# Four score banks, 512-column up products, and the key stack's reads on GpSimd's queue

## The chip, the cores and the metric

The kernel runs on one core of a Trainium2 chip. The metric is the device time of one execution in microseconds (us), the median of several runs. The core's engines each work through their own instructions in order: TensorE (PE, matrix products into eight banks of PSUM), VectorE (DVE), ScalarE (ACT), GpSimd (POOL) and SyncE (SP, which here only issues transfers). They wait for each other by semaphores.

## The reference

Sixteen sequences of 256 tokens, 256 wide, pass through four layers, each conditioned on a vector of 64 per sequence:

```python
h = gamma * rmsnorm(x) + beta                       # layer 0, attention, 16 heads of width 16
o = softmax(scale * q @ k.T) @ v
x = x + alpha * (o @ W_o.T)
x = x + f_alpha * (silu(h2 @ gate.T) * (h2 @ hidden.T) @ out_w.T + out_b)
u = (x * (scale * rsqrt(ms + eps))) @ up_w.T        # layer 1, up product 256 -> 2048
val, gate = split(u)
x = quantised(val * gelu(gate)) @ ternary(down_w).T + x
x = x + relu(x @ Wd_b + bd) @ Wu_b + bu             # layer 2, adapter with per-sequence weights
x = layernorm(x) * w + b, with tanh(cond @ lin_w) added   # layer 3
```

## The kernel before

Each sequence is one batch of the program, and three batches are in flight: `run(a, f, g, nxt)` does the attention of batch a, the feed-forward part and the up product of batch f = a - 1, and the down product, adapter and layer norm of batch g = a - 2; it also prepares q, k and v of batch nxt = a + 1. Every engine has its own `run` with the same four arguments. The order of work on each engine is written out by hand, and `whole` calls `run` for batches 0, 1 and 2, then in a loop for 3 to 14, then for 15, and then `drain`. I call one `run` a pass.

On TensorE a pass is: eight gate products (L650, 12 matmuls each), with the max products (L593), the output products (L664) and the transposes of the quantised rows (L706) between them; then the score stage: down products (L713), 16 heads of scores (L609, two matmuls of 256 columns a head), norm_g (L674) and four attends (L619, 16 small matmuls for four heads), with the pieces of batch g (L720, L727, L733) and `project_v` of nxt (L576) between; then q and k of nxt (L567), mean (L553), output projection (L627), means (L553, L636), `project_v` (L576) again; then eight groups of the up product (L695, 12 matmuls of 256 columns each: two halves, three products, two chunks).

A head's scores go to one of three banks (`SCORE_BANKS`, chosen by h % 3), and ScalarE turns them into probabilities (`exps`, L1005) in one of seven slots. So head h waits for the exponential of head h - 3, attend t for the exponentials of heads 4t to 4t + 3, and the exponential of a head from 7 on for an attend that gives its slot free:

```python
if h >= 3:
    pe.wait_ge(s_exp.sem, s_exp.at(b, h - 2))
...
if h >= SLOTS:
    act.wait_ge(pv_mm.sem, pv_mm.at(b, (h - SLOTS) // 4 + 1))
```

VectorE normalises the attended values in two halves (`normalise`, L1323 to L1331, and `normalised`, L1337 to L1341): half 0 after attends 0 and 1, half 1 after attends 2 and 3. `relu` (L1474) of batch g stands ahead of half 0. In the up product, group n waits for VectorE's `gated_u` (L1411) of group n - 2, since two banks take turns.

q and k are split into a high and a low part and go through memory: SyncE's `stack_qk` writes `q_dram` and `k_dram` (L332), waits until both are there, and reads them back in another layout, six transfers for `q_stack` (L345) and six for `k_stack` (L353), of 128 rows of 1 KB each. Behind them on SyncE stand the output of batch g (L410), which waits for GpSimd's `layer_out` (L472 to L477), and the loads of the next pass (x_in at L317 and others). GpSimd's pass is: eight differences `act_lo` (L495), the adapter's weights (L511), `layer_out`.

Of the kernel before, what the change touches and what calls it, by code (L numbers as in the profile page):

```python
# [22 lines left out]
P = 128  # L23
# [12 lines left out]
SCORE_BANKS = (0, 1, 5)  # L36
# [42 lines left out]
def build(nc, xT, condT, w_cond, w_qkvT, w_oT, w_ghT, w_outT, out_b, w_upT, w_downT,  # L79
          w_hyper, head_rows, adapt_w, adapt_b, bd, bu, ln_w, ln_b, lin_b, ident_in, out):  # L80
    with ExitStack() as ctx:
# [149 lines left out]
        qk_dram_w, stack_dma = sem("qk_dram_w", 32), sem("stack_dma", 16 * 14)  # L231
# [78 lines left out]
        with nc.Block() as block:  # L310

            @block.sync
            def _(sp):
# [7 lines left out]
                def stack_qk(b):  # L321

                    for x, dram in enumerate((q_dram, k_dram)):
# [3 lines left out]
                        if b.follows():  # L327
                            left_value = known(sp, stack_dma.at(b, back=1))
                            sp.wait_ge(stack_dma.sem, left_value)
# [16 lines left out]
                    for a in range(2):  # L346
                        even = slice(64 * a, 64 * a + 32, 2)
                        odd = slice(64 * a + 1, 64 * a + 32, 2)
                        third = slice(64 * a + 32, 64 * a + 64, 2)
                        for rows_at, part in ((even, 0), (odd, 0), (third, 1)):  # L350
                            src = k_dram[:, part].rearrange("(m a r) n -> a r m n", a=2, r=DH)[a]
                            to = k_stack[rows_at].rearrange("r (m a) n -> r a m n", a=2)[:, a]
                            sp.dma_start(to.bitcast(F32), src).then_inc(stack_dma.sem, 16)  # L353
# [113 lines left out]
            def _(pool):  # L467
# [11 lines left out]

                def low_part(n):  # L480
# [7 lines left out]
                def run(a, f, g, nxt):  # L488
# [16 lines left out]
                    if g:  # L505
# [5 lines left out]
                        pool.tensor_tensor(adapt[:], adapt[:], adapt_base[:], ALU.add).then_inc(adapt_w_ready.sem, 1)  # L511
                        layer_out(g)
# [30 lines left out]
                pool.wait_ge(stack_dma.sem, stack_dma.at(Batch(0)))  # L543
                for n in range(2, 10):
                    hyper_load(n)
# [4 lines left out]
            def _(pe):  # L550
# [29 lines left out]
                def max_scores(b, n):  # L580
                    pair, qt = n // 2, n % 2
                    if n == 0:
                        pe.wait_ge(stack_dma.sem, stack_dma.at(b))

# [17 lines left out]
                def scores(b, h):  # L602
# [3 lines left out]
                    if h >= 3:  # L606
                        pe.wait_ge(s_exp.sem, s_exp.at(b, h - 2))
                    for k in range(TT):
                        mm = pe.matmul(halves(SCORE_BANKS[h % 3])[:, k, :], k_stack[:, h, k * P:(k + 1) * P], q_stack[:, h // 2, :],  # L609
                                       start=True, stop=True)  # L610
# [67 lines left out]
                def up(b, n):  # L678
# [11 lines left out]
                    at = halves(7 - n % 2)  # L690
                    for x in range(2):
                        i = 0
                        for w, h in ((up_hi, h3_hi), (up_lo, h3_hi), (up_hi, h3_lo)):
                            for d in range(DC):
                                mm = pe.matmul(at[:, x, :], h[:, d, t * P:(t + 1) * P],  # L695
                                               w[:, d, x * F + c * UW:x * F + (c + 1) * UW], start=(i == 0), stop=(i == 5))
                                i += 1
# [63 lines left out]
                def run(a, f, g, nxt):  # L761
# [46 lines left out]
                    for t in range(4):  # L808
                        if a:
                            if t == 2 and f:  # L810
                                pe.wait_ge(n3_dve.sem, n3_dve.at(f))
                            if t < 3:
                                scores(a, 4 * t + 5)
                                scores(a, 4 * t + 6)
                            elif nxt:
                                project_v(nxt, 0)
# [7 lines left out]
                        if a:  # L824
                            for h in range(4 * t + 7, min(4 * t + 9, H)):
                                scores(a, h)
# [129 lines left out]
            def _(act):  # L956
# [42 lines left out]
                def exps(b, h):  # L999
# [5 lines left out]
                    act.activation(probs[:, h % SLOTS], halves(SCORE_BANKS[h % 3]), ACT.Exp, scale=float(H / D) ** 0.5).then_inc(s_exp.sem, 1)  # L1005
# [116 lines left out]
                def run(a, f, g, nxt):  # L1122
                    if starts(a):
                        act.wait_ge(stack_dma.sem, stack_dma.at(a))
# [655 lines left out]
```

## Time and profile before

| | |
|---|---|
| time, median of 3 runs | 1068.99 us (1067.8 to 1069.29) |
| the profiled execution | 1068.02 us, of which the span of the trace is 1066.2 us |
| TensorE busy | 993.7 us, 93% of the span, 7442 matmuls |
| TensorE weight loads | 848.0 us, 80% |
| VectorE, ScalarE, GpSimd busy | 750.6 us (70%), 553.9 us (52%), 192.7 us (18%) |
| mean granted clock of TensorE | 0.96 of full speed; full in the loop |
| the chain that ended last, by engine | PE 74%, issue 9%, DVE 6%, ACT 4%, DMA 3% |

A row of a timeline has its start in us from the span's start, its length in us, the engine, the line of the kernel, the operation, what it writes and reads (program names), how many instructions it merges (x), and in brackets the idle time before it with what ended it. Matmuls are pipelined, and their ends are modelled: a row's length is longer than what it costs the next one, so the distance from one start to the next is the thing to read. "PE" rows are matmuls; "SPq" rows are transfers as SyncE issues them.

### The profile page before, as it was taken

How to read it: one execution, taken by the hardware profiler on the slowest of the kernel's cores; microseconds unless marked ns; L12 is line 12 of the kernel's file. 1: busy time of each engine (PE TensorE's matmuls, PEld its weight loads, DVE VectorE, ACT ScalarE, POOL GpSimd, SP SyncE). 2: the span in 40 equal slices, each digit the busy share in tenths (PEclk: the TensorE clock that was granted, in tenths of full speed). 3: DMA queues.
4: the chain of work that ended last, by engine and by line, in shares of the span. 5: the costliest groups of instructions: out<-in, count | busy, mean ns of one | idle time of the engine just before them, and what ended most of it. 6: DMA issues, size and time to landing. Idle time of an engine off the chain costs nothing.

```text
span 1066.2 us, 22449 instructions
## 1 busy us (share of the span) xinstructions
PE 993.7 (93%) x7442; PEld 848.0 (80%) x7442; DVE 750.6 (70%) x1720; ACT 553.9 (52%) x1166; POOL 192.7 (18%) x246
## 2 busy tenths in 40 slices
PE   5586989999999999999999999999999999998995
PEld 4244759798898979798988979797988979796984
DVE  3725468676777778686777878686767778785645
ACT  3163364655555464656555463646555564645532
POOL 1411421112020201111120201021120202021220
PEclk9576989999999999999999999999999999999997
DMA  8994543040402113040403112030404022130000
GB/s 287 287 343 129 208 149 91 2 140 2 132 8 90 49 45 94 1 139 1 139 1 110 29 62 77 23 116 1 139 1 129 11 80 60 40 90 2 21 21 10
DMA packets 78321, 89.45 MB, mean 84 GB/s; under 512 B 18688, under 2 KB 64912, under 8 KB 75664
## 3 DMA queue, kind: packets, MB, share of 16 engines
q1 hardware_dynamic: 72640, 63.86, 20.1%
q0 software_dynamic: 2304, 16.78, 4.3%
q10 hardware_dynamic: 3344, 8.39, 2.2%
q8 instruction: 19, 0.31, 0.1%
q14 instruction: 14, 0.11, 0.0%
HBM read 63.14 MB, written 25.31 MB: 83 GB/s over the span
## 4 chain that ended last, share of the span: by engine, by line
PE 74%; issue 9%; DVE 6%; ACT 4%; DMA 3%; POOL 1%; SPq 1%; ACTq 0%; DVEq 0%; POOLq 0%
PE bank L695 15%; PE bank L650 15%; PE bank L664 7%; PE bank L619 6%; PE bank L609 5%; PE bank L593 5%; PE bank L567 4%; PE bank L553 3%; PE bank L713 2%; PE bank L576 2%; ACT probs L1005 2%; PE bank L756 2%; PE bank L636 1%; PE bank L727 1%; PE bank L674 1%
## 5 line engine op out<-in xcount | busy, mean ns | idle before, releaser
L1005 ACT ACTIVATE probs<-bank 128x512 f32<-128x512 f32 x256 | 139.6, 598 | 54.9 <-PE bank L609 54.1
L1306 DVE TENSOR_REDUCE neg_max<-bank 128x2 f32<-128x512 f32 x256 | 161.8, 680 | 0.5 <-PE bank L593 0.5
L495 POOL TENSOR_TENSOR act_lo<-act_f,act_hi 128x256 fp32r<-128x256 f32 x120 | 89.7, 753 | 393.4 <-ACT act_hi L1048 393.4
L1042 ACT ACTIVATE silu_g<-bank 128x256 f32<-128x256 f32 x128 | 49.2, 385 | 192.6 <-PE bank L650 192.4
L1084 ACT ACTIVATE gelu_g<-bank,r 128x256 f32<-128x256 f32 x128 | 60.8, 475 | 95.6 <-PE bank L695 94.8
L609 PE MATMUL bank<-q_stack,k_stack 128*128 128x256 f32 x512 | 99.0, 317 | 11.9 <-ACT probs L1005 11.0
L695 PE MATMUL bank<-up_hi,h_hi 128*128 128x256 f32 x512 | 108.7, 294 | 0.9 <-DVE y L1279 0.3
L650 PE MATMUL bank<-h_hi,gh_hi 128*128 128x256 f32 x512 | 103.7, 284 | 4.6 <-DVE h_lo L1367 4.6
L650 PE MATMUL bank<-h_lo,gh_hi 128*128 128x256 f32 x512 | 103.3, 283 | 0.0
L695 PE MATMUL bank<-up_lo,h_hi 128*128 128x256 f32 x512 | 103.1, 283 | 0.0
L650 PE MATMUL bank<-h_hi,gh_lo 128*128 128x256 f32 x512 | 102.9, 283 | 0.0
L695 PE MATMUL bank<-up_hi,h_lo 128*128 128x256 f32 x512 | 100.7, 278 | 0.0
L1373 DVE TENSOR_TENSOR act_f<-bank,silu_g 128x256 f32<-128x256 f32 x128 | 53.5, 418 | 62.9 <-ACT silu_g L1042 62.9
L609 PEld LDWEIGHTS bank<-q_stack,k_stack 128*128 128x128 f32 x512 | 73.8, 196 | 29.1 <-ACT probs L1005 21.7
L593 PE MATMUL bank<-k_stack,q_stack 128*128 128x512 f32 x256 | 87.6, 429 | 8.9 <-DMA k_stack<-k_dram 6.8
L650 PEld LDWEIGHTS bank<-h_hi,gh_hi 128*128 128x128 f32 x512 | 82.0, 190 | 11.7 <-issue 8.3
L1411 DVE TENSOR_TENSOR act_u<-bank,gelu_g 128x256 f32<-128x256 f32 x128 | 54.1, 422 | 48.1 <-ACT gelu_g L1084 46.1
L472 POOL TENSOR_TENSOR xc<-xc,y 128x512 f32<-128x512 f32 x15 | 19.4, 1295 | 362.2 <-DVE y L1279 362.2
L695 PEld LDWEIGHTS bank<-up_hi,h_hi 128*128 128x128 f32 x512 | 79.3, 189 | 5.3 <-DVE act_u L1411 3.5
L695 PEld LDWEIGHTS bank<-up_lo,h_hi 128*128 128x128 f32 x512 | 79.8, 192 | 0.0
L695 PEld LDWEIGHTS bank<-up_hi,h_lo 128*128 128x128 f32 x512 | 79.2, 190 | 0.0
L650 PEld LDWEIGHTS bank<-h_hi,gh_lo 128*128 128x128 f32 x512 | 79.1, 190 | 0.0
(190 smaller groups left out, 2138.6 us busy)
## 6 DMA issues: line engine op xcount, KB each, us to landing
hyper<-w_hyper POOLq DMA_DIRECT2D x16, 1024.0 KB, 6.5
q_stack<-q_dram SPq DMA_DIRECT2D x96, 128.0 KB
k_stack<-k_dram SPq DMA_DIRECT2D x96, 128.0 KB
q_dram<-probs SPq DMA_DIRECT2D x16, 512.0 KB, 2.8
k_dram<-probs SPq DMA_DIRECT2D x16, 512.0 KB, 3.6
x_res<-xT SPq DMA_DIRECT2D x16, 256.0 KB, 2.8
x_in<-xT SPq DMA_DIRECT2D x15, 256.0 KB, 2.7
out<-xc SPq DMA_DIRECT2D x15, 256.0 KB, 2.5
```

The costliest lines, as they stand in the source:

```text
L495: pool.tensor_tensor(act_lo[:, c % 3, :], act_f[:, c % 2, :], act_hi[:, c % 3, :].bitcast(F32), ALU.subtract).then_inc(g_lo.sem, 1)
L593: pe.matmul(bank[n % 3][:], q_stack[:, pair, qt * P:(qt + 1) * P], k_stack[:, 2 * pair:2 * pair + 2, :], start=True, stop=True).then_inc(m ...
L609: mm = pe.matmul(halves(SCORE_BANKS[h % 3])[:, k, :], k_stack[:, h, k * P:(k + 1) * P], q_stack[:, h // 2, :], start=True, stop=True)
L619: mm = pe.matmul(at[32 * j:32 * j + 32, t % 2, :], v_aug[:, k, 4 * t + j, :], probs[:, (4 * t + j) % SLOTS, k, :], start=(k == 0), stop=(k ...
L650: mm = pe.matmul(at[:, x, :], w[:, d, x * F + c * P:x * F + (c + 1) * P], h[:, d, :], start=(n == 0), stop=(n == 5))
L664: mm = pe.matmul(halves(3)[:, m, :], w[:, c, m * P:(m + 1) * P], h[:, c % 3, :], start=(c == 0 and m == 0 and n == 0), stop=(c == FC - 1 a ...
L695: mm = pe.matmul(at[:, x, :], h[:, d, t * P:(t + 1) * P], w[:, d, x * F + c * UW:x * F + (c + 1) * UW], start=(i == 0), stop=(i == 5))
L1005: act.activation(probs[:, h % SLOTS], halves(SCORE_BANKS[h % 3]), ACT.Exp, scale=float(H / D) ** 0.5).then_inc(s_exp.sem, 1)
L1084: act.activation(gelu_g[:, n % 2, :], halves(7 - n % 2)[:, 1, :], ACT.Gelu, scale=r3[:, t:t + 1])\
L1306: dve.tensor_reduce(neg_max[:, qt, :, pair:pair + 1].rearrange("p a o -> p (a o)"), halves(n % 3), AX_X, ALU.max, negate=True).then_inc(ma ...
L1373: dve.tensor_tensor(act_f[:, c % 2, :], halves(4 + c % 2)[:, 1, :], silu_g[:, c % 2, :], ALU.mult)\
L1411: dve.tensor_tensor(act_u[:, t, c * UW:(c + 1) * UW], halves(7 - n % 2)[:, 0, :], gelu_g[:, n % 2, :], ALU.mult).then_inc(u_dve.sem, 1)
```

## The change

Five edits go together.

1. The up product's two halves (values and gates) become one matmul of 512 columns, whose moving operand is two runs of 256 columns. A group has 6 matmuls and not 12.
2. Scores use four banks: a table gives each head its bank (0, 1, 5 for the first six heads, then 4 as well). From head 7 on a head waits for the exponential of head h - 4 (before: h - 3); head 6 waits until VectorE has read bank 4 in the norm of batch nxt. Heads 5 to 7 go ahead of attend 0, 8 to 11 ahead of attend 1, 12 to 15 ahead of attend 2.
3. From batch 1 on the six reads of `k_stack` are issued by GpSimd (`read_k`), behind the adapter's weights and ahead of `layer_out`, after a small operation and waits for the last scores of batch a and for both writes to memory. Batch 0's stay with SyncE, with a semaphore of their own.
4. SyncE's writes of q_dram and k_dram wait for the last max product of the batch before instead of for the stack's reads.
5. VectorE's `relu` stands inside `normalise(a, 0)`, behind the shuffle.

```diff
-SCORE_BANKS = (0, 1, 5)
+SCORE_BANKS = (0, 1, 5, 0, 1, 5, 4, 0, 1, 5, 4, 0, 1, 5, 4, 0)
...
+            def stack_k(eng, count):
+                for a in range(2):
+                    even = slice(64 * a, 64 * a + 32, 2)
+                    odd = slice(64 * a + 1, 64 * a + 32, 2)
+                    third = slice(64 * a + 32, 64 * a + 64, 2)
+                    for rows_at, part in ((even, 0), (odd, 0), (third, 1)):
+                        src = k_dram[:, part].rearrange("(m a r) n -> a r m n", a=2, r=DH)[a]
+                        to = k_stack[rows_at].rearrange("r (m a) n -> r a m n", a=2)[:, a]
+                        eng.dma_start(to.bitcast(F32), src).then_inc(count.sem, 16)
...
-                            left_value = known(sp, stack_dma.at(b, back=1))
-                            sp.wait_ge(stack_dma.sem, left_value)
+                            left_value = known(sp, max_mm.at(b, back=1))
+                            sp.wait_ge(max_mm.sem, left_value)
...
+                    if not b.follows():
+                        stack_k(sp, first_k_dma)
...
+                def read_k(b):
+                    pool.wait_ge(s_mm.sem, s_mm.at(b, back=1))
+                    pool.wait_ge(qk_dram_w.sem, qk_dram_w.at(b))
+                    pool.tensor_tensor(pool_idle, pool_idle, pool_idle, ALU.mult)
+                    stack_k(pool, k_stack_dma)
...
+                    if nxt:
+                        read_k(nxt)
+                    if g:
                         layer_out(g)
...
+                        if b.follows():
+                            pe.wait_ge(k_stack_dma.sem, k_stack_dma.at(b, back=1))
...
-                    if h >= 3:
-                        pe.wait_ge(s_exp.sem, s_exp.at(b, h - 2))
+                    if h >= 3 and h != 6:
+                        pe.wait_ge(s_exp.sem, s_exp.at(b, h - (2 if h < 6 else 3)))
+                    if h == 6 and nxt:
+                        pe.wait_ge(n1_dve.sem, n1_dve.at(nxt, 4))
                     for k in range(TT):
-                        mm = pe.matmul(halves(SCORE_BANKS[h % 3])[:, k, :], k_stack[:, h, k * P:(k + 1) * P], q_stack[:, h // 2, :],
+                        mm = pe.matmul(halves(SCORE_BANKS[h])[:, k, :], k_stack[:, h, k * P:(k + 1) * P], q_stack[:, h // 2, :],
...
-                    at = halves(7 - n % 2)
-                    for x in range(2):
-                        i = 0
-                        for w, h in ((up_hi, h3_hi), (up_lo, h3_hi), (up_hi, h3_lo)):
-                            for d in range(DC):
-                                mm = pe.matmul(at[:, x, :], h[:, d, t * P:(t + 1) * P],
-                                               w[:, d, x * F + c * UW:x * F + (c + 1) * UW], start=(i == 0), stop=(i == 5))
-                                i += 1
+                    i = 0
+                    for w, h in ((up_hi, h3_hi), (up_lo, h3_hi), (up_hi, h3_lo)):
+                        for d in range(DC):
+                            both = w[:, d, :].rearrange("p (x f) -> p x f", x=2)[:, :, c * UW:(c + 1) * UW]
+                            mm = pe.matmul(halves(7 - n % 2), h[:, d, t * P:(t + 1) * P], both, start=(i == 0), stop=(i == 5))
+                            i += 1
...
-                            if t < 3:
-                                scores(a, 4 * t + 5)
-                                scores(a, 4 * t + 6)
-                            elif nxt:
+                            if t == 0:
+                                for h in range(5, 8):
+                                    scores(a, h, nxt)
+                            elif t == 3 and nxt:
                                 project_v(nxt, 0)
                             attend(a, t)
...
-                        if a:
-                            for h in range(4 * t + 7, min(4 * t + 9, H)):
+                        if a and t < 2:
+                            for h in range(4 * t + 8, 4 * t + 12):
                                 scores(a, h)
...
+                    if between:
+                        relu(between)
```

How the edits move instructions is shown at two places. The first is TensorE in the loop's score stage, from the stage's norm to attend 2. Before (L609 scores, L619 attend, L720, L727, L733 pieces of batch g; a head of scores is two matmuls; products in full precision, the attend's among them, are listed here with half the number that the trace has, 8 for 16):

```order
L609 MATMUL bank<-q_stack,k_stack 128x256 x4
L619 MATMUL bank<-probs,v_aug 32x256 x8
L720 MATMUL bank<-ident,mlp_y 128x128 x4
L609 MATMUL bank<-q_stack,k_stack 128x256 x8
L619 MATMUL bank<-probs,v_aug 32x256 x8
L724 REGISTER_ALU
L727 MATMUL bank<-x,adapt 128x256 x2
L609 MATMUL bank<-q_stack,k_stack 128x256 x4
L811 REGISTER_ALU
L609 MATMUL bank<-q_stack,k_stack 128x256 x4
L619 MATMUL bank<-probs,v_aug 32x256 x8
L733 MATMUL bank<-adapt_h,adapt 128x256 x2
```

After (L630 scores, L640 attend, L739, L746, L752 the same pieces):

```order
L630 MATMUL bank<-q_stack,k_stack 128x256 x2
L628 ISA
L630 MATMUL bank<-q_stack,k_stack 128x256 x4
L640 MATMUL bank<-probs,v_aug 32x256 x8
L739 MATMUL bank<-ident,mlp_y 128x128 x4
L630 MATMUL bank<-q_stack,k_stack 128x256 x8
L640 MATMUL bank<-probs,v_aug 32x256 x8
L743 REGISTER_ALU
L746 MATMUL bank<-x,adapt 128x256 x2
L630 MATMUL bank<-q_stack,k_stack 128x256 x8
L830 REGISTER_ALU
L640 MATMUL bank<-probs,v_aug 32x256 x8
```

One head more stands ahead of attend 0, and the last head, which stood behind L733, now stands ahead of attend 2; the other heads are the same four between two attends.

The second place is GpSimd at the end of its pass in the loop. Before (L511 adapter's weights, L472 to L477 `layer_out`):

```order
L495 TENSOR_TENSOR act_lo<-act_f,act_hi 128x256 x2
L510 ISA
L511 TENSOR_TENSOR adapt<-adapt,adapt_base 128x512
L471 ISA
L472 TENSOR_TENSOR xc<-xc,y 128x512
L474 ISA
L475 TENSOR_TENSOR columns<-columns 128x1
L477 TENSOR_SCALAR xc<-xc,neg_w,par_g 128x256 x2
```

After (L522 adapter's weights, L321 the reads of k, L477 to L482 `layer_out`):

```order
L506 TENSOR_TENSOR act_lo<-act_f,act_hi 128x256 x2
L521 ISA
L522 TENSOR_TENSOR adapt<-adapt,adapt_base 128x512
L486 ISA
L487 ISA
L488 TENSOR_TENSOR columns<-columns 128x1
L321 DMA k_stack<-k_dram 16x8x256 x6
L476 ISA
L477 TENSOR_TENSOR xc<-xc,y 128x512
L479 ISA
L480 TENSOR_TENSOR columns<-columns 128x1
L482 TENSOR_SCALAR xc<-xc,neg_w,par_g 128x256 x2
```

Two waits, a small operation and six transfers stand between the adapter's weights and `layer_out`. SyncE has lost the same six.

## Rows read from the trace of the kernel before

**Rows 1.** TensorE's timeline: the first max products of two neighbouring passes.

```profile
528.64 0.86 PE L593 MATMUL bank<-k_stack,q_stack 128*128 128x512 f32 x3
...
588.02 0.85 PE L593 MATMUL bank<-k_stack,q_stack 128*128 128x512 f32 x3
```

**Rows 2.** TensorE's timeline in the score stage of the same pass.

```profile
554.11 0.72 PE L609 MATMUL bank<-q_stack,k_stack 128*128 128x256 f32 x4
554.76 1.07 PE L619 MATMUL bank<-probs,v_aug 128*32 128x256 f32 x16
...
556.17 0.96 PE L609 MATMUL bank<-q_stack,k_stack 128*128 128x256 f32 x6
557.42 0.50 PE L609 MATMUL bank<-q_stack,k_stack 128*128 128x256 f32 x2 [0.29 <-ACT probs L1005]
557.85 1.07 PE L619 MATMUL bank<-probs,v_aug 128*32 128x256 f32 x16
558.85 1.13 PE L727 MATMUL bank<-x,adapt 128*128 128x256 f32 x4
559.63 1.05 PE L609 MATMUL bank<-q_stack,k_stack 128*128 128x256 f32 x6
560.98 0.50 PE L609 MATMUL bank<-q_stack,k_stack 128*128 128x256 f32 x2 [0.30 <-ACT probs L1005]
561.42 1.07 PE L619 MATMUL bank<-probs,v_aug 128*32 128x256 f32 x16
...
564.58 1.07 PE L619 MATMUL bank<-probs,v_aug 128*32 128x256 f32 x16
565.58 3.72 PE L567 MATMUL bank<-h,w_qkv 128*128 128x256 f32 x16
```

**Rows 3.** ScalarE's timeline in the same stage.

```profile
560.33 0.60 ACT L1005 ACTIVATE probs<-bank 128x512 f32<-128x512 f32 x1 [1.11 <-PE bank L609]
...
561.23 1.56 ACT L1005 ACTIVATE probs<-bank 128x512 f32<-128x512 f32 x3
562.66 0.43 ACT L1009 ACTIVATE den_y<-den 128x256 f32<-128x256 f32 x1
```

**Rows 4.** VectorE's timeline in the same pass.

```profile
552.66 0.69 DVE L1288 TENSOR_TENSOR h<-x_in,bank 128x512 f32<-128x512 f32 x1
...
560.42 0.48 DVE L1323 TENSOR_SCALAR den_raw<-bank,rows_of 128x256 f32<-128x256 f32 x1
...
565.72 0.48 DVE L1323 TENSOR_SCALAR den_raw<-bank,rows_of 128x256 f32<-128x256 f32 x1
...
578.95 0.42 DVE L1411 TENSOR_TENSOR act_u<-bank,gelu_g 128x256 f32<-128x256 f32 x1
...
580.46 0.70 DVE L1367 TENSOR_TENSOR h_lo<-h,h_hi 128x512 fp32r<-128x512 f32 x1
```

**Rows 5.** The chain that ended last: start, length, matmuls of 256 and of 512 columns.

```profile
527.38 1.43 PE bank L650 x12
528.81 0.70 PE bank L593 x3
```

**Rows 6.** SyncE's queue, as it issues the reads of q and the next x_in.

```profile
575.93 3.88 SPq L345 DMA_DIRECT2D q_stack<-q_dram  x6
...
584.92 0.40 SPq L317 DMA_DIRECT2D x_in<-xT  x1
```

**Rows 7.** GpSimd's timeline: four issues at the start, and the output stage of the pass.

```profile
39.60 2.15 POOL L532 DMA_DIRECT2D hyper<-w_hyper  x4 [1.78 <-DMA k_stack<-k_dram]
...
575.75 1.29 POOL L472 TENSOR_TENSOR xc<-xc,y 128x512 f32<-128x512 f32 x1 [25.29 <-DVE y L1279]
```

**Rows 8.** VectorE's timeline at the start, while GpSimd works too.

```profile
39.57 0.48 DVE L1722 TENSOR_SCALAR adapt_bias<-w_early,w_stats 128x512 f32<-128x512 f32 x1
...
80.45 1.37 DVE L1339 SCALAR_TENSOR_TENSOR den_x<-den_x,den_y 128x256 f32<-128x256 f32 x1
```

**Rows 9.** ScalarE's timeline: the first use of x_in in the next pass.

```profile
590.68 0.62 ACT L958 ACTIVATE h<-x_in 128x512 f32<-128x512 f32 x1
```

**Rows 10.** The page's list of transfers: issues, KB each, us to landing.

```profile
x_in<-xT SPq DMA_DIRECT2D x15, 256.0 KB, 2.7
```

More of the change, by code:

```diff
@@ L230, in build @@
         x_in_dma, x_res_dma = sem("x_in_dma", 32), sem("x_res_dma", 32)
-        qk_dram_w, stack_dma = sem("qk_dram_w", 32), sem("stack_dma", 16 * 14)
+        qk_dram_w, stack_dma = sem("qk_dram_w", 32), sem("stack_dma", 16 * 8)
+        first_k_dma, k_stack_dma = sem("first_k_dma"), sem("k_stack_dma", 16 * 6)
         max_dma = sem("max_dma", 32)
@@ L345, in stack_qk @@
                             sp.dma_start(q_stack[rows_at].bitcast(F32), src).then_inc(stack_dma.sem, 16)
[L346 to L353, printed above, removed]
+                    if not b.follows():
+                        stack_k(sp, first_k_dma)
                 def load_res(b):
@@ L543, in _ @@
                 pool.wait_ge(stack_dma.sem, stack_dma.at(Batch(0)))
+                pool.wait_ge(first_k_dma.sem, 16 * 6)
                 for n in range(2, 10):
@@ L583, in max_scores @@
                         pe.wait_ge(stack_dma.sem, stack_dma.at(b))
+                        if b.follows():
+                            pe.wait_ge(k_stack_dma.sem, k_stack_dma.at(b, back=1))
+                        else:
+                            pe.wait_ge(first_k_dma.sem, 16 * 6)
                     if n == 0:
@@ L600, in max_turn, with scores @@
                     mm.then_inc(max_t.sem, 1)
-                def scores(b, h):
+                def scores(b, h, nxt=None):
                     if h == 0:
@@ L1004, in exps @@
                         act.wait_ge(pv_mm.sem, pv_mm.at(b, (h - SLOTS) // 4 + 1))
-                    act.activation(probs[:, h % SLOTS], halves(SCORE_BANKS[h % 3]), ACT.Exp, scale=float(H / D) ** 0.5).then_inc(s_exp.sem, 1)
+                    act.activation(probs[:, h % SLOTS], halves(SCORE_BANKS[h]), ACT.Exp, scale=float(H / D) ** 0.5).then_inc(s_exp.sem, 1)
                 def den_guess(b, u):
@@ L1124, in run @@
                         act.wait_ge(stack_dma.sem, stack_dma.at(a))
+                        act.wait_ge(first_k_dma.sem, 16 * 6)
                         raw_load(2)
@@ L1307, in row_max, with normalise @@
                                       negate=True).then_inc(max_red.sem, 1)
-                def normalise(b, u):
+                def normalise(b, u, between=None):
                     k = 8 * u
@@ L1525, in run @@
                         norm_g(f)
-                    if g:
+                    if g and not a:
                         relu(g)
@@ L1531, in run @@
                     if a:
-                        normalise(a, 0)
+                        normalise(a, 0, g)
                     if starts(a):
```

## Prediction

> **What bounds the kernel now.** I read the page first (TensorE is the full engine), then TensorE's timeline through one pass of the loop, then ScalarE's, VectorE's and the queues' at the same place. The passes in the middle look alike, so one stands for all: the first wide max product of two neighbouring passes starts at 528.64 and 588.02, a period of 59.4 us [rows 1]. TensorE is the bound, but it isn't always working. From the first attend (554.76) to the projection L567 (565.58) it spends 10.82 us [rows 2]. The reader is to see two holes there, at 557.42 and 560.98, each ended by ScalarE's exponential. The brackets give 0.29 and 0.30 us, but the ends of matmuls are modelled; by starts, the three heads from 556.17 (six matmuls of 0.12) were through by 556.9 and the next one began at 557.42. ScalarE itself waits at the same places, because head 7 is issued only behind attend 0 and the transpose L720 (and head 11 behind attend 1 and L727): each engine idles in turn for the other. With three banks TensorE can't run far enough ahead to fill this.
>
> **The score order.** Distances between starts give block lengths [rows 2]: attend 1.00 (557.85 to 558.85), L727 0.78, L720 0.41 (from 554.76 to 556.17 less an attend), two heads of scores with their start-up 0.65, each further head 0.24, so four heads some 1.1. From attend 2 to attend 3 it is 3.16: an attend, head 15 (0.41), and 1.75 for L733 and L576. I lay the new order on the clock of this pass:
> - heads 5, 6, 7 from 554.11 take 0.89: attend 0 at 555.00 (0.24 later than before), L720 at 556.00;
> - heads 8 to 11 from 556.41: attend 1 at 557.50 (before 557.85), L727 at 558.50;
> - heads 12 to 15 from 559.28: attend 2 at 560.4 (before 561.42);
> - L733 and L576, then attend 3 at 563.15 (before 564.58), L567 at 564.15 (before 565.58).
> That is 1.4 to 1.5, and I take 1.5, since blocks that now adjoin lose some of the start-up that I counted twice.
>
> Is ScalarE there in time? Exponentials in a row come every 0.48 (three in 1.56) and L1075 between adds 0.4 (560.33 to 561.23) [rows 3]. Head 11's needs attend 1 to be over, 558.6. Then L1075 and, once head 12 is there (about 559.8), three exponentials until 561.3, the pair L1009/L1011 (two of 0.43) until 562.2, and the last until 562.8. Attend 3 at 563.15 finds it done, with 0.3 spare. VectorE: the first normalisation starts when attend 1 is over, 558.6 instead of 560.42, 1.8 earlier; the relu that now stands inside it adds 0.4 to 0.5, as L1323's 0.48. So the second (5.30 after the first [rows 4]) starts 1.3 to 1.4 earlier, about when attend 3 is over. What is late next is therefore VectorE's chain, by 0.1 or 0.2; TensorE has L567 and L553 to do before it needs the result, so I let the 1.5 pass. The new wait of head 6 on bank 4 is for L1288, the last reader of that bank, which ends at 553.35 [rows 4], before 554.11: nothing.
>
> **The up products.** 96 matmuls of 256 columns become 48 of 512 per batch. Twelve of 256 take 1.43, 0.119 each; three of 512 with new weights each take 0.70, 0.233 each [rows 5]. A pair of 0.238 becomes 0.233: 48 x 0.005, or 0.24 to 0.3 per batch. The fourth group of products waits for VectorE's L1411, which ends at 579.37 [rows 4] at the end of VectorE's own chain of norms. So what the first three of eight groups save is given back there: 0.2 per pass are left. The Trainium skill (TensorE: Matmul & The Clock Gate, Back-to-back issue gap) gives a gap of N/2.4 + 2.5 ns, by which a pair saves only 2.5 ns. By it this term would be 0.1 in place of 0.2, and the whole some 1 us slower; the rows show 0.119 and 0.233, both above its 0.109 and 0.216, so I stay with the rows.
>
> **The key reads.** SyncE now issues 6 reads of q (3.88 us from 575.93) and not 12; six of k go to GpSimd, with a small operation ahead, and the output stage L472 and its followers stand behind them there. Nothing waits for the stack in the loop: the twelfth read was out by 583.7, and the first product that needs them starts at 588.02 with no idle before it [rows 1]. So taking them away from SyncE brings nothing by itself; the question is whether GpSimd's issues hurt. The trace has no k read from GpSimd. Nearest row: four of the 1 MB hyper loads in 2.15, 0.54 each [rows 7]. The bound from above: SyncE takes 0.65 for a q read and 0.40 for x_in [rows 6], so the finer pattern may cost 1.6 times as much, 0.9. I take 0.54 to 0.9, near the first because both are 128 rows. From 574.6 (575.93 less 1.5, plus the small operation) six end at 577.8 to 580.0. Behind them wait L472 (at 575.75 before), L475 and L477, 2.6 in all (L472 1.29 of it [rows 7]), so xc is ready at 580.5 to 582.6, not 578.4. Who waits for that is SyncE, with the output and behind it x_in, which was issued at 584.92. SyncE itself has 3.8 us of reads fewer ahead of it, so x_in goes out at 582 to 584, not later than now in the pass. ScalarE wants it at 590.68 [rows 9]. Cost: nothing. If GpSimd takes 1.35 per issue, that cover is gone: 574.6 + 8.1 + 2.6 + 1.0 for output and x_in, and 2.7 to land [rows 10] is 589.0, its new due time (590.68 less 1.7).
>
> **Sum.** 13 passes with all three batches in flight, 1.7 each: 22.1. The passes of batches 0, 1 and 15 have the same four attends, but hyper products, table loads or VectorE's chain between: 1.5 each, 4.5; their up products and those of the drain, 0.3 each, 0.9. Batch 1's k reads in the start land earlier by some 3 us, but gate products stand ahead of their use: 0. Together 27.5 from 1068.0 of the profiled execution (1.0 under the median of the runs): 1040.5, and 1041 for the median.
>
> **Rivals.**
> - Collision on VectorE's and GpSimd's port, chance 0.13. At 80.45 a VectorE operation with two inputs from the tile memory took 1.37 for 256 elements (L1323 takes 0.48), about as long as GpSimd's own operations, one of which was in flight [rows 8]. L1367 (580.46 [rows 4], so 579.0 in the new pass) is of that kind. If the issues cost 0.65 to 0.85, L472 starts just ahead of it, its 1.29 hold it up, and the product of up group 3 behind it comes 0.65 late, so TensorE stops: 13 x 0.65 = 8.5, 1049. Outside this span of costs L472 falls before or after it.
> - The stall only moves, chance 0.12: ScalarE or VectorE, with 0.3 and nothing spare, end the stage later than laid out, and 0.9 of the 1.5 is left. 16 x 0.9 + 3.5 = 18, 1050.
> - GpSimd's issues are slow: slower than before, chance 0.06. From 1.35 each on, every 0.1 costs 0.6 per pass; at 1.65 the 1.7 is used up and it decides. At 2.0 it is 2.1 x 13 = 27 over, 1095. Against it stands the 0.54 row, and that VectorE kept to 0.48 for L1722 right then (39.57) [rows 8]. The Trainium skill (SBUF — State Buffer, the "DVE blocks DMA" trap) says that VectorE's fast modes keep GpSimd from writing descriptors; if that rule bites it is this case, and in the rows of 39.57 and 39.60 it doesn't.
> - The change doesn't do what it says, chance 0.03: what ends the stage is the chain of norms and the reorder is absorbed, 1067 to 1069.
> - Better than laid out, chance 0.06: the start-ups of the score blocks go too, 2.0 per pass, and up keeps all of its 0.3: 13 x 2.3 + 6 = 36, 1032.
>
> **How the numbers follow.** The likeliest case, chance 0.60, gives 1041, by itself 1036 to 1046. The range for 8 in 10 takes in the two rivals of 1049 and 1050 and not the far ones: 1034 to 1052. Faster by over 0.2% (about 2 us, what a measurement of this kernel can tell from none) is all but the slow issues, part of which is still a gain, and the fourth case: 0.90. Same 0.04, slower 0.06.
>
> **What would show it.** Right: passes of 57.7; L609 with no idle before it by ScalarE; four attends closer, L567 some 9.2 after attend 0; the up matmuls of 512 every 0.23; GpSimd's six issues within 3.2 to 5.4 us. Wrong: an idle of TensorE ahead of L553 or the up products that VectorE ends (rivals 1 and 2); ScalarE waiting for x_in, or the first max product for k_stack (rival 3). My forecast fails most easily in the cost of GpSimd's issues and in ScalarE's 0.3 us of slack.

## The result, and the profile after

The changed kernel took **1052.14 us** (median of 4 runs, 1048.5 to 1052.55) and the kernel before 1068.65 beside it: ratio 0.9832, 95% interval 0.9811 to 0.9852. That is 16.5 us faster. The profiled execution took 1052.55, with a span of 1051.0. I had forecast 27.5 us of gain, so the direction is right and the size is not: 11 us are missing. The time lies at the slow end of my range (1034 to 1052).

The page of the changed kernel, busy time of each engine and the lines on scores, products and transfers:

```profile
PE 983.8 (94%) x6674; PEld 803.0 (76%) x6674; DVE 753.2 (72%) x1720; ACT 554.0 (53%) x1166; POOL 247.3 (24%) x351
...
L630 PE MATMUL bank<-q_stack,k_stack 128*128 128x256 f32 x512 | 84.8, 304 | 3.5 <-ACT probs L1024 3.5
...
k_stack<-k_dram POOLq DMA_DIRECT2D x90, 128.0 KB, 4.9
...
x_in<-xT SPq DMA_DIRECT2D x15, 256.0 KB, 3.7
out<-xc SPq DMA_DIRECT2D x15, 256.0 KB, 4.1
```

Scores now wait 3.5 us for exponentials in the whole run; 11.0 of the 11.9 us of idle that L609 had before were ended so. The lines have new numbers: L609 is L630, attend L619 is L640, L567 is L582, L576 is L591, L727 and L733 are L746 and L752, the up products L695 are L715, the exponentials L1005 are L1024, the output stage L472 is L477.

TensorE's timeline: the first max products of two neighbouring passes, and the first gate products of batch 1 and of batch 14, between which lie all 13 passes with three batches in flight:

```profile
172.69 0.40 PE L671 MATMUL bank<-h_hi,gh_hi 128*128 128x256 f32 x2
...
522.99 0.87 PE L612 MATMUL bank<-k_stack,q_stack 128*128 128x512 f32 x3
...
581.15 0.87 PE L612 MATMUL bank<-k_stack,q_stack 128*128 128x512 f32 x3
...
928.96 0.40 PE L671 MATMUL bank<-h_hi,gh_hi 128*128 128x256 f32 x2
```

The period is 58.16 here, where it was 59.38 [rows 1]. The 13 passes take 756.27, or 58.17 each. The same two products stand in the trace of before at:

```profile
171.28 0.40 PE L650 MATMUL bank<-h_hi,gh_hi 128*128 128x256 f32 x2
...
943.00 0.40 PE L650 MATMUL bank<-h_hi,gh_hi 128*128 128x256 f32 x2
```

That is 771.72, or 59.36 each. So a pass is 1.19 shorter and 13 of them 15.4, where I had 22.1. All but about 1 us of the measured gain is there.

TensorE's timeline of the changed kernel in the score stage (it answers to [rows 2]):

```profile
548.45 0.96 PE L630 MATMUL bank<-q_stack,k_stack 128*128 128x256 f32 x6
549.34 1.07 PE L640 MATMUL bank<-probs,v_aug 128*32 128x256 f32 x16
550.34 0.66 PE L739 MATMUL bank<-ident,mlp_y 128*128 128x128 f32 x4
550.75 1.19 PE L630 MATMUL bank<-q_stack,k_stack 128*128 128x256 f32 x8
551.88 1.07 PE L640 MATMUL bank<-probs,v_aug 128*32 128x256 f32 x16
552.88 1.13 PE L746 MATMUL bank<-x,adapt 128*128 128x256 f32 x4
553.66 1.30 PE L630 MATMUL bank<-q_stack,k_stack 128*128 128x256 f32 x8
554.88 1.07 PE L640 MATMUL bank<-probs,v_aug 128*32 128x256 f32 x16
555.88 1.13 PE L752 MATMUL bank<-adapt_h,adapt 128*128 128x256 f32 x4
556.85 1.03 PE L591 MATMUL bank<-w_qkv,h 128*128 128x256 f32 x4
557.81 1.07 PE L640 MATMUL bank<-probs,v_aug 128*32 128x256 f32 x16
558.81 3.72 PE L582 MATMUL bank<-h,w_qkv 128*128 128x256 f32 x16
```

The reader is to see the four attends 2.54, 3.00 and 2.93 apart and no bracket anywhere: the trace shows no wait of TensorE here. Yet the stage, from attend 0 to L582, is 9.47 and not the 9.2 that I named.

ScalarE's timeline at its end:

```profile
554.28 1.58 ACT L1024 ACTIVATE probs<-bank 128x512 f32<-128x512 f32 x3 [0.27 <-PE bank L630]
...
556.51 0.58 ACT L1024 ACTIVATE probs<-bank 128x512 f32<-128x512 f32 x1
```

The last exponential is through at 557.09, 0.7 ahead of attend 3. ScalarE is not what made the stage longer than I laid it out.

GpSimd's timeline, from the key reads to the output stage, and SyncE's queue at the same time:

```profile
569.20 0.19 POOL L488 TENSOR_TENSOR columns<-columns 128x1 f32<-128x1 f32 x1 [24.41 <-DMA k_dram<-probs]
569.33 3.24 POOL L321 DMA_DIRECT2D k_stack<-k_dram  x6
572.58 1.31 POOL L477 TENSOR_TENSOR xc<-xc,y 128x512 f32<-128x512 f32 x1
573.96 0.53 POOL L480 TENSOR_TENSOR columns<-columns 128x1 f32<-128x1 f32 x1
```

```profile
569.15 3.88 SPq L356 DMA_DIRECT2D q_stack<-q_dram  x6
575.76 0.40 SPq L415 DMA_DIRECT2D out<-xc  x1
576.72 0.40 SPq L328 DMA_DIRECT2D x_in<-xT  x1
```

Six issues in 3.24, 0.54 each, and x_in goes out at 576.72 where it is first wanted at 583.83 (a row of ScalarE's timeline, below).

```profile
583.83 0.62 ACT L977 ACTIVATE h<-x_in 128x512 f32<-128x512 f32 x1
```

### The profile page after: what moved, and what is told of

Same layout as the page of the kernel before. It is cut to its first block, busy times and chain, and to the rows that moved or that the text cites. A ratio compares the mean times of both kernels' runs of the same rounds, so it can differ in the third digit from the quotient of the medians.

```text
span 1051.0 us, 20966 instructions
## 1 busy us (share of the span) xinstructions
PE 983.8 (94%) x6674; PEld 803.0 (76%) x6674; DVE 753.2 (72%) x1720; ACT 554.0 (53%) x1166; POOL 247.3 (24%) x351
## 4 chain that ended last, share of the span: by engine, by line
PE 75%; DVE 8%; issue 7%; DMA 5%; ACT 2%; POOL 1%; SPq 1%; ACTq 0%; DVEq 0%; POOLq 0%
PE bank L671 16%; PE bank L715 13%; PE bank L685 8%; PE bank L630 6%; PE bank L640 6%; PE bank L612 5%; PE bank L582 5%; PE bank L568 3%; PE bank L732 3%; PE bank L591 2%; PE bank L695 1%; PE bank L746 1%; PE bank L752 1%; PE bank L775 1%; DMA par_a<-cond_dram 1%
## 5 line engine op out<-in xcount | busy, mean ns | idle before, releaser
L1024 ACT ACTIVATE probs<-bank 128x512 f32<-128x512 f32 x256 | 139.7, 598 | 28.3 <-PE bank L630 22.5
L630 PE MATMUL bank<-q_stack,k_stack 128*128 128x256 f32 x512 | 84.8, 304 | 3.5 <-ACT probs L1024 3.5
L715 PE MATMUL bank<-up_hi,h_hi 128*128 128x512 f32 x256 | 87.1, 422 | 1.1 <-DVE act_u L1433 0.2
L488 POOL TENSOR_TENSOR columns<-columns 128x1 f32<-128x1 f32 x15 | 2.9, 193 | 346.5 <-DMA k_dram<-probs 346.5
L715 PE MATMUL bank<-up_lo,h_hi 128*128 128x512 f32 x256 | 80.3, 395 | 0.0
L715 PE MATMUL bank<-up_hi,h_lo 128*128 128x512 f32 x256 | 80.3, 395 | 0.0
L671 PEld LDWEIGHTS bank<-h_lo,gh_hi 128*128 128x128 f32 x512 | 79.1, 189 | 0.0
L630 PEld LDWEIGHTS bank<-q_stack,k_stack 128*128 128x128 f32 x512 | 69.2, 195 | 12.2 <-ACT probs L1024 7.1
L685 PE MATMUL bank<-act_hi,fo_hi 128*128 128x256 f32 x256 | 75.5, 295 | 0.9 <-POOL act_lo L506 0.7
L685 PE MATMUL bank<-act_hi,fo_lo 128*128 128x256 f32 x256 | 71.4, 279 | 0.0
```

What stands on the lines that cost most here:

```text
L630: mm = pe.matmul(halves(SCORE_BANKS[h])[:, k, :], k_stack[:, h, k * P:(k + 1) * P], q_stack[:, h // 2, :], start=True, stop=True)
L671: mm = pe.matmul(at[:, x, :], w[:, d, x * F + c * P:x * F + (c + 1) * P], h[:, d, :], start=(n == 0), stop=(n == 5))
L685: mm = pe.matmul(halves(3)[:, m, :], w[:, c, m * P:(m + 1) * P], h[:, c % 3, :], start=(c == 0 and m == 0 and n == 0), stop=(c == FC - 1 a ...
L715: mm = pe.matmul(halves(7 - n % 2), h[:, d, t * P:(t + 1) * P], both, start=(i == 0), stop=(i == 5))
L1024: act.activation(probs[:, h % SLOTS], halves(SCORE_BANKS[h]), ACT.Exp, scale=float(H / D) ** 0.5).then_inc(s_exp.sem, 1)
```

## The experiments

Single executions of one kernel lie up to 8.5 us apart, so each kernel is read in two ways: its ratio to the kernel before on the same chip, and the 13 passes in its trace (first gate product of batch 1 to that of batch 14). The second is far sharper: three traces of the changed kernel give 756.27, 756.31 and 756.48, so a difference of 0.02 us in a pass can't be told from none. In the table, "A" is the time up to that first product (it holds the attends of batches 0 and 1) and "C" what follows the last (it holds those of batch 15).

| kernel | ratio (95% interval) | A | 13 passes | one pass | C |
|---|---|---|---|---|---|
| before | 1 | 171.3 | 771.7 | 59.36 | 123.2 |
| e1, up products alone | 0.9993 (0.9981 to 1.0006) | 171.6 | 770.6 | 59.27 | 124.5 |
| e2, score part alone | 0.9850 (0.9825 to 0.9876) | 170.7 | 757.5 | 58.27 | 121.5 |
| e3, key reads alone | 0.9993 (0.9981 to 1.0006) | 171.8 | 772.0 | 59.38 | 122.9 |
| e4, up and scores | 0.9826 (0.9805 to 0.9847) | 171.0 | 756.1 | 58.16 | 121.1 |
| e11, e4 again | 0.9836 (0.9809 to 0.9862) | 173.0 | 756.0 | 58.15 | 123.5 |
| after | 0.9832 (0.9811 to 0.9852) | 172.7 | 756.3 | 58.17 | 122.0 |
| e5, after again | 0.9844 (0.9820 to 0.9868) | 172.7 | 756.3 | 58.18 | 122.0 |
| e12, after again | 0.9830 (0.9801 to 0.9860) | 172.0 | 756.5 | 58.19 | 123.7 |
| e10, first keys on SyncE | 0.9815 (0.9790 to 0.9841) | 170.5 | 756.5 | 58.19 | 122.7 |
| e7, e4 with three banks | 1.0002 (0.9984 to 1.0019) | 172.1 | 771.1 | 59.32 | 122.6 |
| e8, e4 in the old order | 0.9866 (0.9843 to 0.9888) | 171.7 | 759.6 | 58.43 | 122.6 |
| e9, e4 with relu ahead | 0.9876 (0.9851 to 0.9900) | 171.7 | 759.4 | 58.42 | 122.7 |
| e6, e4 with the modulations split off | 0.9790 (0.9762 to 0.9818) | 172.0 | 752.4 | 57.88 | 123.1 |

**e1: the up products alone.** The kernel before with only this hunk:

```
-                    for x in range(2):
-                        ...
-                                mm = pe.matmul(at[:, x, :], h[:, d, t * P:(t + 1) * P],
+                            both = w[:, d, :].rearrange("p (x f) -> p x f", x=2)[:, :, c * UW:(c + 1) * UW]
+                            mm = pe.matmul(halves(7 - n % 2), h[:, d, t * P:(t + 1) * P], both, start=(i == 0), stop=(i == 5))
```

> The kernel before with the 512-wide up products alone. My term for this part was 0.3 x 16 = 4.5 at most and 0.2 per pass at the least, so 3 to 4.5 us of gain. The trace of the changed kernel shows only 0.09 us per pass gained between the first up product and the next gate, because more up groups now wait for VectorE's gated product: by that theory (VectorE eats the gain) this kernel is 1 to 2 us faster than before, 1067. Rival, the gain is all there and was given back elsewhere in the changed kernel: 4 us, 1064.5.

1068.44 against 1068.83, and 0.09 us per pass. The rival (the whole gain of 4 us) is out: the interval ends at 2 us.

**e2: the score part alone.** The kernel before with the bank list, the waits, the order of heads and attends, and the relu of the diff; nothing else.

```
-SCORE_BANKS = (0, 1, 5)
+SCORE_BANKS = (0, 1, 5, 0, 1, 5, 4, 0, 1, 5, 4, 0, 1, 5, 4, 0)
-                    if g:
+                    if g and not a:
                         relu(g)
```

> The kernel before with four score banks, the new order of scores and attends, and relu moved behind the shuffle; up products stay 256 wide and all stack reads stay on SyncE's queue. Theory: this part alone is what the change gained, 1.1 us in each of 14 to 15 batches (15 to 17 us), so 1052 to 1054, with the period 58.25 to 58.3. Rival, the start of the run lost 1.5 to 3 us to the key reads that ran beside the query reads: then this kernel has what the changed kernel has in its loop and does not pay that, 1050 to 1052.

1052.04, and 1.10 us per pass, as expected. This part is the gain.

**e3: the key reads alone.** From batch 1 on they are issued by GpSimd, and SyncE's writes have the new wait (edit 4); scores, banks, relu and up products as before.

```
+                    if nxt:
+                        read_k(nxt)
+                    if g:
                         layer_out(g)
```

> The kernel before with the key reads from batch 1 on issued from GpSimd's queue, nothing else. Theory from the prediction: nothing, 1068 to 1069. Rival: batch 1's query stack lands 7.1 us after its issue (so in the changed kernel's trace) because the key reads run beside it, and the maxima of batch 1 start some 2 us later: 1070 to 1071, with the loop's period unchanged at 59.4.

1068.61 against 1068.83, and 0.02 us per pass more, about as much as traces of one kernel differ. The interval of this run, start and end of the run included, leaves the key reads a cost of at most 0.6 us beside the old scores; the rival (1.2 to 2.2 us) is out. The three parts add up: 0.09 + 1.10 - 0.02 = 1.17, and the changed kernel has 1.19.

**e4: up and scores, keys on SyncE.** The changed kernel with this undone:

```
-                    if nxt:
-                        read_k(nxt)
+                    for a in range(2):
+                        ...
+                            sp.dma_start(to.bitcast(F32), src).then_inc(stack_dma.sem, 16)
```

> The changed kernel with its key reads left on SyncE's queue: wide up products and the score part. If the key reads cost nothing it takes what the changed kernel took, 1052 within 0.5. If they cost the start of the run some 2 us, it takes 1050.

1050.09, which looked like 2 us for the key reads. The passes say otherwise (58.16 and 58.17); what differs is A and C. That was put to the test with the next runs.

**e5, e11, e12 and e10: do the key reads cost anything at the ends?** e5 and e12 are the changed kernel, e11 is e4 once more on the chip of e12, and e10 gives back to SyncE only the reads of batch 1:

```
-                    if not b.follows():
+                    if b.early():
                         stack_k(sp, first_k_dma)
...
-                    if nxt:
+                    if nxt and not nxt.early():
                         read_k(nxt)
```

> The changed kernel itself once more, beside the other runs of this group. The kernel with the same wide products and score part but the key reads on SyncE took 1050.1, this one took 1052.1, on different chips. If the key reads cost the start of the run, it stays at 1052, with the second batch's last gate stage (the third in the run) starting 1.5 to 2 us later (172.7 against 171.0). If that was only the run's own variation, 1050 to 1051.

> Wide up products and the score part with the key reads on SyncE, once more, on the same chip as the changed kernel. If the key reads on GpSimd cost something, 1050 again and the changed kernel 2 to 3 us above it; if the difference was between chips, both the same within 0.5.

> The changed kernel beside it: 1052 to 1053.5 if the key reads cost something, else as the one with the keys on SyncE within 0.5.

> The changed kernel with the second batch's key reads issued by SyncE as before; GpSimd reads the keys from the third batch on. The changed kernel took 1052.1 and 1053.5, with the keys on SyncE 1050.1. Theory: the difference is made at the second batch, where the input of the next batch, behind the query reads, landed 7.0 us after its issue and not 3.0: this kernel takes 1050 to 1051. Rival: it is made in the end or is variation, and this kernel takes what the changed kernel takes beside it.

1053.48 for e5, whose first gate product of batch 1 stands at 172.67 as in the first trace of this kernel. That looked like the theory, but e11, with the keys on SyncE, has it at 173.01. On one chip the medians are 1050.63 (e10), 1051.98 (e11) and 1052.82 (e12). The last two differ by 0.8, with intervals of the ratio that overlap almost wholly: no cost of the key reads that these runs can tell from none. e10 is lower than e12 as the first theory had it, by 2.2 us, but e11 has those reads on SyncE as well and is lower by only 0.8; the interval of e10 overlaps both. With the new scores, a cost of a microsecond at batch 1 is neither shown nor excluded.

What is seen to differ with A and C, between traces of one kernel, is the granted clock. Two traces of one and the same kernel, e4 and e11, by windows (stretch, its length and busy TensorE with its instructions, then the granted clock):

```profile
960.00:970.00 10.00, 6.58 (x49) 0.94 0.01 2
970.00:980.00 10.00, 9.59 (x35) 0.89 0.08 27
```

```profile
960.00:970.00 10.00, 6.59 (x61) 0.92 0.01 2
970.00:980.00 10.00, 9.64 (x29) 0.74 0.00 1
```

Both have full clock (2.4 GHz) up to 960 and lose it around the stretch in which TensorE worked 6.6 of 10 us; e11 gets less of the next ten at full clock, and its C is 2.4 us longer. By these two rows 1.5 us of that can be the clock (an estimate: 0.15 of ten us). A goes the same way: from 100 to 110 us the clock is 0.83 in e4 and 0.66 in e11, from 140 to 150 it is 0.87 and 0.71. In e11 the projection of batch 0 stands 0.8 us earlier (89.90 against 90.71), the first scores of batch 1 0.8 later (135.20 against 134.37) and its projection 2.0 later (157.22 against 155.19).

**e7: three banks in the new order.** e4 with

```
-SCORE_BANKS = (0, 1, 5, 0, 1, 5, 4, 0, 1, 5, 4, 0, 1, 5, 4, 0)
+SCORE_BANKS = (0, 1, 5)
-                    if h >= 3 and h != 6:
-                        pe.wait_ge(s_exp.sem, s_exp.at(b, h - (2 if h < 6 else 3)))
+                    if h >= 3:
+                        pe.wait_ge(s_exp.sem, s_exp.at(b, h - 2))
```

> The same but with only three score banks in the new order of heads and attends. Theory: the fourth bank is what makes the new order work. From the exponentials' ends, head 7 would wait 0.1, head 11 0.5 and head 15 0.4 us for the exponential three heads back, 1.0 us per batch: 1064 to 1066, a period of 59.2. Rival, the order alone brings the gain: 1050 to 1052.

1068.13 against 1068.47: nothing is left of the gain, where I had expected 0.16 us of each pass to stay (59.32 and not 59.2). TensorE's timeline shows the holes back, now ahead of heads 11 and 15 (in the kernel before, ahead of 10 and 14):

```profile
557.20 0.96 PE L609 MATMUL bank<-q_stack,k_stack 128*128 128x256 f32 x6
558.46 0.50 PE L609 MATMUL bank<-q_stack,k_stack 128*128 128x256 f32 x2 [0.30 <-ACT probs L1003]
558.90 1.07 PE L619 MATMUL bank<-probs,v_aug 128*32 128x256 f32 x16
...
560.68 1.05 PE L609 MATMUL bank<-q_stack,k_stack 128*128 128x256 f32 x6
561.95 0.50 PE L609 MATMUL bank<-q_stack,k_stack 128*128 128x256 f32 x2 [0.22 <-ACT probs L1003]
```

**e8: four banks in the old order.** e4 with the heads issued in pairs again:

```
-                            if t == 0:
-                                for h in range(5, 8):
-                                    scores(a, h, nxt)
+                            if t < 3:
+                                scores(a, 4 * t + 5, nxt)
+                                scores(a, 4 * t + 6, nxt)
```

> The same with four score banks but the old order of heads and attends. Theory: TensorE's two holes of 0.3 us (ahead of heads 9 and 13) close, since these heads no longer wait for an exponential that has just begun; the time that ScalarE idles for heads 7 and 11 stays: half of the gain, 0.5 to 0.6 us per batch, 1057 to 1059. Rival, the idle of ScalarE decides and the attends stay where they were: 1066.

1055.10 and 58.43 per pass. Less the 0.09 of the up products, 0.84 of the score part's 1.10 is there (with the relu in its new place), more than I expected. The order is worth the other 0.27, and by itself, with three banks (e7), nothing. The holes that close are those ahead of heads 10 and 14, not 9 and 13 as the expectation has it. In this kernel ScalarE's timeline keeps two idles, ahead of the exponentials of heads 7 and 11, that the new order removes:

```profile
551.59 0.60 ACT L1005 ACTIVATE probs<-bank 128x512 f32<-128x512 f32 x1 [0.67 <-PE bank L611]
...
554.72 0.60 ACT L1005 ACTIVATE probs<-bank 128x512 f32<-128x512 f32 x1 [0.68 <-PE bank L611]
```

**e9: relu ahead of the first normalisation.** e4 with

```
-                    if g and not a:
+                    if g:
                         relu(g)
...
-                        normalise(a, 0, g)
+                        normalise(a, 0)
```

> Wide up products, four banks, new order, key reads on SyncE, and VectorE's relu back ahead of the first normalisation. There it waits for the product L727, which ends 1.0 us after attend 1, so the reciprocal's input is ready 1.0 later. ScalarE issues the last exponential behind that reciprocal; it ends at 555.34 where attend 3 begins at 556.06, 0.72 of slack. Theory: attend 3 comes 0.2 to 0.3 later, 3 to 4 us in all, 1053 to 1054, with the period 58.4. Rival: the slack takes it, 1050.

1055.48, 58.42 per pass, 0.26 longer: the size in a pass is as expected, the reason is not. TensorE's and VectorE's timelines:

```profile
556.31 1.13 PE L733 MATMUL bank<-adapt_h,adapt 128*128 128x256 f32 x4
557.46 1.10 PE L576 MATMUL bank<-w_qkv,h 128*128 128x256 f32 x4
558.49 1.07 PE L621 MATMUL bank<-probs,v_aug 128*32 128x256 f32 x16
```

```profile
556.83 0.48 DVE L1333 SCALAR_TENSOR_TENSOR o_norm<-bank,rows_of,o_norm 128x256 f32<-128x256 f32 x1
```

The last exponential still ends (557.80) 0.7 ahead of attend 3. It is L576 that is late. It writes bank 2, which the normalisation reads until L1333 is over (557.31), and L576 starts 1.15 after L733, where it is 0.97 in e4 (554.13 to 555.10). With relu inside (e4), L1333 was over 1.0 us ahead of L576.

**e6: the modulations split off.** e4, with the two modulations behind the normed x1 moved behind VectorE's second gated product:

```
+                def modulated_f(b):
                     dve.wait_ge(n2_dve.sem, n2_dve.at(b, 4))
...
                         if a and n == 0:
                             scaled_f(a)
+                        if a and n == 1:
+                            modulated_f(a)
```

> Wide up products and the score part with the key reads on SyncE, and on VectorE the two modulations behind the normed x1 moved behind the second gated product of the up stage. Theory: the fourth up group is late by 0.27 us and the fifth by 0.1 because the second gated product stands behind all three operations (570.40 where its Gelu ended at 569.88). Freed, each pass is 0.3 shorter: 57.9 instead of 58.2, and 4 to 5 us in all, 1045.5 to 1046.5. Rival: the next product waits for something else in its place (ScalarE's pair of copies, then its rounded copy), 1050.

1048.52, 57.88 per pass: 0.28 shorter, as expected, and the fastest kernel of the study, 2.1% under before. The whole time is 2 us above the 1045.5 to 1046.5 that I expected, since I counted from e4's 1050.09; e11, the same kernel as e4, took 1051.98 on another chip. Below, TensorE's timeline of the changed kernel at the start of its third, fourth and fifth up group, and of e6 at the same three:

```profile
570.96 0.69 PE L715 MATMUL bank<-up_hi,h_hi 128*128 128x512 f32 x2
...
572.63 0.73 PE L715 MATMUL bank<-up_hi,h_hi 128*128 128x512 f32 x2
...
574.13 0.62 PE L715 MATMUL bank<-up_hi,h_hi 128*128 128x512 f32 x2
```

```profile
568.75 0.69 PE L696 MATMUL bank<-up_hi,h_hi 128*128 128x512 f32 x2
...
570.20 0.61 PE L696 MATMUL bank<-up_hi,h_hi 128*128 128x512 f32 x2
...
571.57 0.63 PE L696 MATMUL bank<-up_hi,h_hi 128*128 128x512 f32 x2
```

1.67 and 1.50 apart in the one, 1.45 and 1.37 in the other. What held the fourth group was VectorE's second gated product, which stood behind three operations on h2.

## Why the prediction was right in sign and 11 us off in size

- **What bounds, and that the holes close.** Right. Both holes of 0.3 are gone, two of 0.30 and 0.22 come back when the fourth bank is taken away (e7), and the score part by itself makes the gain (e2).
- **"I take 1.5."** Mis-sized, and the main error: the score stage gives 1.10 per pass (e2), and 0.4 times 13 is 5.2 us. I laid the stage out with block lengths from other neighbourhoods, and the timeline after shows which were short. Heads 12 to 15 took 1.22 (553.66 to 554.88), heads 8 to 11 1.13, where I had "some 1.1". L752 to L591 took 0.97 where I used 0.78, the length of a block like it with scores behind it; with L591 at 0.96 my 2.75 for attend 2 to attend 3 became 2.93. Attend 0 came 0.24 later, as said, so the gain in front of L567 is that from attend 0 on, 1.35, less 0.24: 1.11. My own layout gave 1.43; the rest was my rounding up to 1.5 with a reason (start-up counted twice) that had the wrong sign. Of the blocks that now adjoin, none got shorter here, and two got longer.
- **ScalarE in time with 0.3 to spare.** Right, with 0.7 to spare.
- **VectorE's chain late by 0.1 or 0.2, hidden by L567 and L553.** In a pass of the loop it is 4.42 from L567 to the projection L627 in both traces (565.58 to 570.00 before, 558.81 to 563.23 after): hidden. What I didn't see is what the relu's place is worth. I priced it inside the normalisation as 0.4 to 0.5 on a covered chain; ahead of it, it would have held L591 through bank 2, 0.26 per pass (e9).
- **Up products, "0.24 to 0.3 per batch", 0.2 in a pass.** Mis-sized. In the traces a group of up products that waits for nothing takes 1.41 before (576.38 to 577.79) and 1.39 after (569.57 to 570.96), so eight give 0.16. I had taken 0.119 from the gate products' row; those of the up stage were 0.1175 apart. Of the 0.16, 0.07 is given back, nearly all at the fourth group, whose wait for VectorE grew, as I had said (its predecessor takes 1.67 with that wait, 0.28 over a group without a wait; in the kernel before it took 1.63, 0.22 over). 0.09 is left (e1), 1.4 us less in 13 passes than forecast. The rule of the Trainium skill that the prediction set aside (TensorE: Matmul & The Clock Gate, Back-to-back issue gap) would have given 0.1 and was nearer than my two rows. What it gets right is the difference of a pair; the distances themselves are above it here too (0.1175 and 0.232 for its 0.109 and 0.216).
- **The key reads cost nothing.** Right in the loop (e3: 0.02 per pass; e4 and e11 within 0.02 of the changed kernel), by the mechanism named: 0.54 per issue, x_in out in time. For the start, e3 leaves at most 0.6 us.
- **13 passes at 1.7.** 13 at 1.19: 15.4 and not 22.1.
- **Batches 0, 1 and 15 at 1.5 each.** This was the other step that failed, for batches 0 and 1. From the first scores to the projection, batch 15 takes 18.45 before and 17.27 after, so 1.2 of its 1.5 is there; batch 1 takes 22.6 and 22.1; batch 0 takes 26.0 and 26.6 (25.0 to 26.6 in the other traces, with the old order of heads and the new). In batch 0 TensorE does come sooner from attend 0 to L567 (12.5 us after, 13.5 before), but then it waits for VectorE's normalised values, and longer than before. TensorE's timeline before and after, then VectorE's and GpSimd's after:

```profile
87.38 3.75 PE L627 MATMUL bank<-o_norm,w_o 128*128 128x256 f32 x8 [4.65 <-DVE o_norm L1341]
```

```profile
89.20 3.75 PE L648 MATMUL bank<-o_norm,w_o 128*128 128x256 f32 x8 [5.38 <-DVE o_norm L1363]
```

```profile
82.28 1.37 DVE L1361 SCALAR_TENSOR_TENSOR den_x<-den_x,den_y 128x256 f32<-128x256 f32 x1
...
88.17 0.43 DVE L1361 SCALAR_TENSOR_TENSOR den_x<-den_x,den_y 128x256 f32<-128x256 f32 x1
```

```profile
79.45 5.32 POOL L496 TENSOR_TENSOR fo_lo<-w_raw,fo_hi 128x512 fp32r<-128x512 f32 x4 [4.65 <-ACT fo_hi L1139]
```

One and the same VectorE operation takes 1.37 while GpSimd's L496 runs and 0.43 when it is over. After the change three of these operations in a row take that long (L1359, L1361, L1363: 1.39, 1.37, 1.37), in the kernel before two (L1337 took 0.67). From L567 to the projection it is 9.1 us after and in e2, e4, e10, e11 and e12, 8.4 before and in e1, e3 and e8. My prediction names VectorE's chain here and shows that very row (80.45, [rows 8]), and takes 1.5 all the same.
- **What A and C leave.** In whole stretches, the four traces without the score gain (before, e1, e3, e7) have a mean of 171.7 for A and 123.3 for C, the six with the up and score parts together 172.0 and 122.5. So some 0.5 us is left of the 5.4 that I summed for these batches and their up products. It is no sharp number: A runs from 170.5 to 173.0 within the six, and the three stages above have 1.1 together.
- **Sum.** 15.4 in the passes and 0.5 to 1.1 around them make 16 to 16.5, measured 16.5. Of the missing 11, some 5.2 are the score stage's size, 1.4 the up products' and 4 to 5 the first and last batches, batch 0 above all.
- **The range.** That the time still lies at the edge of 1034 to 1052 is luck: the range reached so far because of the rivals of 1049 and 1050, and neither happened.
- **Rivals.** "The stall only moves" had a time of 1050 and is nearest, but not by its mechanism: neither ScalarE nor VectorE ended the stage; TensorE's own blocks were longer than I laid out. The collision of L1367 with L472 was there in small: L1389 (L1367 before) takes 0.81 after for 0.70 before, and L480 (L475) 0.53 for 0.20, with no loss in a pass. Slow issues on GpSimd are out at 0.54. "The change doesn't do what it says" is out by e2.

## What to carry to other kernels

When a stage is re-ordered on paper, take each block's length from a place in the trace where it has the same neighbours as it will have; 0.1 to 0.2 us in each of two blocks were the difference between 1.4 and 1.1. A new order and a new buffer can each be worth nothing or most of it without the other: try both alone. A gain per pass isn't the gain of the first passes, where another engine may end the stage: look there for the wait that ends last. Where single runs lie up to 0.8% apart, compare a stretch of many equal passes inside two traces; three traces of one kernel agreed within 0.02 us per pass.

## What was not expected of the hardware

- With the key reads on GpSimd's queue, transfers behind the reads take longer from issue to landing: over the whole run the medians are 3.7 for x_in and 4.1 for the output in the changed kernel, and 2.7 and 2.5 before. For x_in this is mostly its earlier issue. In the pass of batch 0, e3 has it issued at 96.57 and landed 7.0 later, the trace of before at 99.84 and 3.0 later: 14.5 and 14.3 us after the write of k_dram (89.11 and 88.52).
- Two traces of one kernel can differ by 2 us in the last 120, with the granted clock of one stretch of ten us at 0.89 in the one and 0.74 in the other.
- VectorE's operation of 256 elements with both inputs in the tile memory takes 1.37 us beside GpSimd's L496 and 0.43 without it.
